# Four latent-cross-attention layers over 64 sequences on one core: masks, padded keys, value matmuls, weight transfers and the order of the work changed

## Chip, cores and metric

One NeuronCore of a Trainium2 chip runs the whole program. The metric is the device time of one execution in microseconds (us). Engines: PE (TensorE, matmul), DVE (VectorE), ACT (ScalarE), POOL (GpSimd), SP (SyncE, which only issues transfers here).

## What is computed

Four layers are applied to x (64 sequences x 64 tokens x 256) with a context of 64 tokens per sequence. Cut to what matters:

```
x = L0(ctx, x, mask)   # 16 heads of 16: softmax(q k) v over ctx and x together (128 keys; the
                       # context's masked keys get no weight), out, + x, norm, gelu MLP, + x
x = L1(x, ctx)         # RWKV block: token shift, five mixes, r k v w g, state scan
                       #   s = k v + w s,  out = r (u k v + s), group norm, gate, feed-forward
x = L2(x, ctx)         # one head of 256: x + alpha * softmax(q k) v Wo
x = L3(x, ctx, amask)  # 32 query heads of 8 on 8 key/value heads, + additive mask, out, + x, norm
```

Everything is float32.

## The kernel before

The 64 sequences are worked in 16 tiles of 4 (256 tokens). Each tile goes through three parts: A (L0), B (the RWKV mixing of L1) and C (the feed-forward of L1, then L2 and L3), as lists of named stages (`STAGES`). The string `ORDER`, written out by hand as 82 letters, says from which part the next stage comes; `AHEAD` lets A work two tiles and B one tile ahead of C. So one iteration of the program holds the stages of A for tile t+2, of B for t+1 and of C for t, mixed as ORDER has them: 18 iterations, the first with A alone, the second with A and B, then 14 with all three, one with B and C, one with C. All five engines walk the same sequence (`run`), each doing its share of each stage in that order and waiting on semaphores for the others. There is no scheduler: where a stage stands in ORDER sets what stands behind a wait on every engine, SP's transfers among them.

PSUM: banks 0 to 3 hold the scores and then the values and sums of both attentions (`max`, `exp`, `value` stages, A and C by turns), banks 4 and 5 belong to B, and banks 6 and 7 are a ring for all dense matmuls of A and C (`USES`, `SLOT`, `spare`, `full`, `read`): a matmul of slot k waits until slot k-2 has been read.

The stages that the text below speaks of:

- `q0`, `k0`, `v0` (L550, 552, 559 on PE): the projections of A. ACT writes `kT` from `k0`.
- `max0` (`max_scores`, L417): scores of two sequences, 16 matmuls in four row groups of 32 rows; then 8 more (L410 `pw<-m,wa`) add `m0`, -1e30 for a masked key, to the first 64 keys. DVE takes maxima (L1112). `turn0` (L578) transposes them, `exp0` makes the scores again, transposed, with -max added; ACT exponentiates (L837) with the mask as bias. `value0` (`values`) makes sums and values, DVE divides (L1117, L1120) to `tA`, `out0` multiplies by the output weights, `norm0` adds x on DVE (L1202), squares on ACT (L887), takes the root on POOL (L1014, L1016) and scales on ACT to `a2` (L891), which `zturn` transposes on PE (L399 `pw<-wa,a`). `up` (L610, four stages, gelu on ACT at L899) and `down` (L616) are the MLP.
- `mix2` (L513): five mixes of part B. Mix j multiplies 32 rows of `thB` in row group f % 4, f = `MIX[j]` = 2, 0, 1, 3, 4, into bank 4 or 5 by turns; DVE finishes each (L1241) and POOL adds (L1052). `mixes(0, 1)` and `mixes(2, 3)` interleave the matmuls of two mixes, `mixes(4)` is alone.
- `ruk`, `scan` 0 to 7, `sum`, `oturn` in B: SP copies v to eight places (`copy_v`), POOL makes the outer products (L1029), DVE scans (L1262), POOL multiplies with r (L1065), PE sums (`gather`).
- `k3`, `v3` in C: keys and values of the third attention, the one of L3. ACT makes four padded copies of the keys for the four places of a head in a group of 32 rows (`kz3`, L987). `v3` multiplies twice (L774), once for each half of the output rows, and DVE copies the heads into padded places. `max1`: PE (L410 `pw<-kz,q3T`), DVE adds the mask (L1108) and takes maxima (L1112). `x3turn` transposes (L399 `pw<-wa,c`), ACT copies to `tC` (L976), `q3` multiplies.

PE itself waits at the start for the weights `wa` and for DVE's preparation of them, whose last step halves `fv` (L1377).

Of the kernel before, what the change touches and what calls it, by code (L numbers as in the profile page):

```python
# [7 lines left out]
I32 = mybir.dt.int32  # L8
# [4 lines left out]
P = 128  # L13
# [19 lines left out]
WEIGHTS_A = [("ident", P), ("q0", 2 * C), ("k0", 2 * C), ("v0", 2 * C), ("o0", 2 * C), ("vec", 64), ("fv", 2 * C), ("ones0", 48), ("ones3", 64), ("pick", 32),  # L33
             ("top", P), ("eye", 32), ("o3", 2 * C)]
# [43 lines left out]
ORDER = "AABACBABCCBCABCABCABBCBBCABBAABABACBACBCBCBBCCBBACBAABBCABABACBBCBBBCBBBACCBACCBCB"  # L78
# [48 lines left out]
def build(nc, h_d, x_d, mask_d, maskt_d, amask_d, s0_d, e0_d, wa_d, wb_d, nat_d, rows_d, out_d):  # L127
# [4 lines left out]
    with ExitStack() as ctx:  # L132
# [249 lines left out]
        def _(pe):  # L382
# [154 lines left out]
            def part_a(name, i, t):  # L537
# [166 lines left out]
            def part_c(name, i, t):  # L704
# [765 lines left out]
```

## Time and profile before

| | before |
|---|---|
| median of 3 runs | 1628.97 us (1628.13 to 1629.14) |
| the profiled execution | 1628.69 us |
| its span, first to last instruction | 1626.5 us |
| mean granted clock of PE | 0.964 of full speed |
| busy: PE, PE weight loads | 1459.5 us (90%), 1119.1 us (69%) |
| busy: DVE, POOL, ACT | 958.1 (59%), 649.4 (40%), 626.7 us (39%) |
| chain that ended last, by engine | PE 71%, DVE 10%, ACT 7%, POOL 7%, issue 3%, DMA 2% |

The span is what the profiler saw between the first and the last instruction; the execution's own time is 2.2 us longer. Busy times of matmuls are modelled and overlap, so the time of a step on PE is better read as the distance from its start to the next start. A timeline row gives the start (us from the span's start), the length of the group, engine, source line, operation, what it writes and reads, its shape and how many records it has (an f32 matmul has two), and in brackets the idle time ahead of it with what ended it.

### The profile page before, as it was taken

Reading aid. Unit: us, or ns where it says so; the run is one execution under the profiler, and the core shown is the slowest. Engines: PE = TensorE matmul, PEld = TensorE weight load, DVE = VectorE, ACT = ScalarE, POOL = GpSimd, SP = SyncE. Lnnn points to the kernel's source line nnn. Section 1 sums busy time; section 2 is a strip of 40 time slices with the busy share of each in tenths; the row PEclk is TensorE's granted clock in tenths of the full one; section 3 lists DMA queues with packets and bytes.
Section 4 is the critical chain, followed back from the end, with each engine's and each line's share of the span. In section 5 each row is a group of like instructions: output and inputs, shape, how many; then the busy total and the mean of one; then the engine's idle time right before and its main releaser. Section 6 shows DMA issues by size and latency. Waiting matters only on the chain.

```text
span 1626.5 us, 45176 instructions
## 1 busy us (share of the span) xinstructions
PE 1459.5 (90%) x19704; PEld 1119.1 (69%) x19704; DVE 958.1 (59%) x1913; ACT 626.7 (39%) x1367; POOL 649.4 (40%) x604
## 2 busy tenths in 40 slices
PE   6777999999999999999999999999899999997664
PEld 4665767777777767777776777777676777775443
DVE  1244576665657576674757666575756656573733
ACT  2332444434343443534344343434344343433221
POOL 1043344525344453525335452533445253443410
PEclk9898999999999999999999999999999999997877
DMA  8021130404022040403113040311304040221300
GB/s 293 11 41 29 22 67 15 77 25 77 25 31 58 16 76 24 77 25 54 34 24 74 18 77 25 70 28 28 65 14 77 25 77 24 34 31 22 49 7 8
DMA packets 83093, 75.27 MB, mean 46 GB/s; under 512 B 37201, under 2 KB 72145, under 8 KB 82513
## 3 DMA queue, kind: packets, MB, share of 16 engines
q1 hardware_dynamic: 82896, 72.39, 22.2%
q8 instruction: 156, 2.56, 0.6%
q14 instruction: 41, 0.33, 0.1%
HBM read 34.61 MB, written 4.19 MB: 24 GB/s over the span
## 4 chain that ended last, share of the span: by engine, by line
PE 71%; DVE 10%; ACT 7%; POOL 7%; issue 3%; DMA 2%; SPq 0%; DVEq 0%; POOLq 0%; ACTq 0%
PE pw L410 21%; PE pw L388 14%; PE pw L394 7%; PE pw L610 6%; PE pw L616 6%; PE pw L559 3%; DVE c L1117 3%; POOL ab L1065 3%; PE pw L513 3%; POOL ab L1029 2%; PE pw L399 2%; PE pw L552 2%; ACT qz L861 2%; PE pw L729 2%; ACT ptC L839 1%
## 5 line engine op out<-in xcount | busy, mean ns | idle before, releaser
L1029 POOL TENSOR_TENSOR ab<-big,kvrg 128x504 f32<-128x504 f32 x128 | 161.2, 1259 | 115.9 <-DMA big<-kvrg 86.3
L1065 POOL TENSOR_TENSOR ab<-ab,kvrg 128x512 f32<-128x512 f32 x128 | 162.7, 1271 | 67.9 <-DVE ab L1262 67.6
L1262 DVE TENSOR_TENSOR_SCAN ab<-pw,ab 128x256 f32<-128x256 f32 x256 | 158.6, 671 | 48.4 <-ACT ab L947 45.9
L1052 POOL TENSOR_TENSOR big<-big,xaB 128x512 f32<-128x512 f32 x80 | 101.4, 1269 | 166.4 <-DVE big L1241 165.2
L610 PE MATMUL pw<-tA,wb 128*128 128x256 f32 x512 | 123.6, 397 | 3.7 <-DVE tA L1206 3.1
L388 PE MATMUL pw<-big,wb 128*128 128x256 f32 x512 | 125.8, 389 | 0.0
L616 PE MATMUL pw<-wb,ptA 128*128 128x256 f32 x512 | 118.1, 384 | 0.0
L1112 DVE TENSOR_REDUCE mx<-pw 128x8 f32<-128x1024 f32 x64 | 75.2, 1216 | 72.3 <-PE pw L410 72.3
L610 PEld LDWEIGHTS pw<-tA,wb 128*128 128x128 f32 x512 | 98.4, 197 | 27.8 <-issue 12.4
L1117 DVE RECIPROCAL a<-pw 128x256 f32<-128x256 f32 x32 | 56.1, 1752 | 103.0 <-PE pw L410 103.0
L616 PEld LDWEIGHTS pw<-wb,ptA 128*128 128x128 f32 x512 | 96.9, 192 | 15.2 <-issue 2.4
L388 PEld LDWEIGHTS pw<-big,wb 128*128 128x128 f32 x512 | 92.1, 190 | 18.9 <-POOL big L1052 4.6
L1014 POOL TENSOR_TENSOR vtmp_A<-mv_A,eps 128x2 f32<-128x2 f32 x16 | 3.2, 197 | 254.5 <-DVE mv_A L1132 254.5
L839 ACT ACTIVATE ptC<-pw 128x1024 f32<-128x1024 f32 x64 | 62.0, 1021 | 88.5 <-PE pw L410 88.5
L837 ACT ACTIVATE ptA<-pw,mk 128x1024 f32<-128x1024 f32 x64 | 67.8, 1111 | 63.1 <-PE pw L410 63.1
L899 ACT ACTIVATE ptA<-pw,wa 128x256 f32<-128x256 f32 x128 | 53.7, 471 | 99.0 <-PE pw L610 99.0
L388 PE MATMUL pw<-tC,wb 128*128 128x256 f32 x256 | 71.7, 428 | 16.6 <-ACT tC L976 13.4
L1241 DVE SCALAR_TENSOR_TENSOR big<-pw,wa,sxB 128x256 f32<-128x256 f32 x160 | 66.8, 475 | 32.5 <-PE pw L513 32.5
L410 PE MATMUL pw<-mT,wa 32*64 32x128 f32 (+1 forms) x3072 | 75.9, 274 | 4.4 <-issue 4.4
L1108 DVE TENSOR_TENSOR ptC<-pw,m 128x1024 f32<-128x1024 f32 x64 | 74.9, 1211 | 7.3 <-PE pw L410 6.8
L1112 DVE TENSOR_REDUCE mx<-ptC 128x16 f32<-128x1024 f32 x64 | 75.0, 1214 | 1.1
L388 PEld LDWEIGHTS pw<-tC,wb 128*128 128x128 f32 x256 | 50.7, 208 | 32.3 <-DVE v3s L1339 14.6
(216 smaller groups left out, 3082.6 us busy)
## 6 DMA issues: line engine op xcount, KB each, us to landing
big<-kvrg SPq DMA_DIRECT2D x256, 128.0 KB, 4.1
hT<-in_h SPq DMA_DIRECT2D x16, 512.0 KB, 4.4
m<-in_amask SPq DMA_DIRECT2D x96, 64.0 KB, 2.3
wb<-in_wb SPq DMA_DIRECT2D x1, 5120.0 KB, 22.6
a<-in_x SPq DMA_DIRECT2D x16, 256.0 KB, 4.2
xB<-in_x SPq DMA_DIRECT2D x16, 256.0 KB, 2.8
result<-c SPq DMA_DIRECT2D x16, 256.0 KB, 2.1
m<-in_mask SPq DMA_DIRECT2D x16, 128.0 KB, 2.5
```

The source lines that it names most:

```text
L388: last = mm(out[:, m, :], weight(k)[:, m * P:(m + 1) * P], rhs(k), start=(k == 0), stop=(k == 1))
L394: last = mm(out[:, t, :], lhs(k, t), weight(k), start=(k == 0), stop=(k == ks - 1))
L410: return mm(out, lhs, rhs, start=first, stop=last, skip_group_check=True)
L610: last = mm(kn(bank(k))[:, m, :], w("w1", c)[:, mt * P:(mt + 1) * P], tA[:, c, :], start=(c == 0), stop=(c == 1))
L616: last = mm(bank(k)[:, 0:C], hid[:, c, tok(i)], w2[:, c, :], start=(c == 0), stop=(c == 7))
L839: last = A(pt[1][p][:, 2 * j:2 * j + 2, :], pw[:, 2 * j:2 * j + 2, :], ACT.Exp)
L1029: G.tensor_tensor(ab[i % 4][:, :, :, 1:S], vx[i % 3].rearrange("p j (b s) -> p j b s", b=NB)[:, :, :, 0:S - 1], k, ALU.mult).then_inc(kv_p ...
L1052: G.tensor_tensor(v, v, xaB[:, :, :, 1:S + 1].rearrange("p k b s -> p (k b) s"), ALU.add).then_inc(xm_ok, 1)
L1065: G.tensor_tensor(ab[i % 4][:, :, :, :], st[i % 2][:, :, :, :], r, ALU.mult).then_inc(pd_ok, 1)
L1112: V.tensor_reduce(mx[:, 2 * j:2 * j + 2, g * p:g * p + g], src[:, 2 * j:2 * j + 2, :].rearrange("p r (g s) -> p r g s", g=g), AXX, ALU.max ...
L1117: V.reciprocal(rc[layer][:, p, :], ps[(1, 2)[p]][:, 0:2 * P]).then_inc(o_rc, 1)
L1262: last = V.tensor_tensor_scan(st[i % 2][:, j, :, :].rearrange("p b s -> p (b s)"), kn(b5)[:, i // 4, :], ab[i % 4][:, j, :, :].rearrange(" ...
```

## The change

Masked keys: in place of adding -1e30 by matmuls, DVE compares the mask (`gone`) and copies over each masked context key in `kT` the key of the first latent position (column S), by a predicated copy. The maximum is then one over real keys; the weights still get their mask in `exp0`. Padded keys: ACT writes one copy `k3S`, POOL makes the four padded ones from it. `v3`: each product is made once, and DVE copies it to both halves, in eight pieces. `mixes` becomes `mix`: the mixes are no longer interleaved. Weights: `wa` comes in two transfers, PE waits for the first only, and no longer for `set_pool` and `set_dve`; the halving of `fv` moves into `fold_weights`. And ORDER is another string.

```diff
-WEIGHTS_A = [("ident", P), ("q0", 2 * C), ("k0", 2 * C), ("v0", 2 * C), ("o0", 2 * C), ("vec", 64), ("fv", 2 * C), ...
+WEIGHTS_A = [("vec", 64), ("q0", 2 * C), ("k0", 2 * C), ("ident", P), ("ones0", 48), ("ones3", 64), ("pick", 32), ("top", P), ("eye", 32),
+             ("v0", 2 * C), ("o0", 2 * C), ("fv", 2 * C), ("o3", 2 * C)]
...
-ORDER = "AABACBABCCBCABCABCABBCBBCABBAABABACBACBCBCBBCCBBACBAABBCABABACBBCBBBCBBBACCBACCBCB"
+ORDER = "AABACBABBCCBBABCCCBCBBCABBBCBABCBBBCACCBAABBCAAACABBBCBABAACBBCABBBCBBBACCBACCACBB"
...
-            sp.dma_start(wa[:, :], wa_d).then_inc(ld_w, 16)
+            sp.dma_start(wa[:, 0:ca["v0"][0]], wa_d[:, 0:ca["v0"][0]]).then_inc(ld_w, 16)
             load_context(0)
+            sp.dma_start(wa[:, ca["v0"][0]:na], wa_d[:, ca["v0"][0]:na]).then_inc(ld_v, 16)
...
-                if layer == 0:
-                    for i in range(2):
-                        b = 2 * p + i
-                        for r in range(4):
-                            last = into(ps[r][:, 256 * i:256 * i + 256].rearrange("p (k s) -> p k s", k=2)[:, :, 0:S], w("top")[group(r), :],
-                                        m0[group(r), b, :].unsqueeze(1).broadcast_to([32, 2, S]), False, i == 1)
...
-            def mixes(*js):
-
+            def mix(j):
+
+                f = MIX[j]
+                g = group(f % 4)
                 for m in range(2):
-                    for j in js:
-                        f = MIX[j]
-                        g = group(f % 4)
-                        last = mm(kn((b4, b5)[j % 2])[:, m, :], w("m2", f // 4)[g, m * P:(m + 1) * P], thB[g, f // 4, :], start=True, stop=True)
-                        if m == 1:
-                            last.then_inc(m2_ps, 1)
+                    last = mm(kn((b4, b5)[j % 2])[:, m, :], w("m2", f // 4)[g, m * P:(m + 1) * P], thB[g, f // 4, :], start=True, stop=True)
+                last.then_inc(m2_ps, 1)
...
-                        pe.wait_ge(*read(SLOT["k0", 0, t]))
-                        pe.wait_ge(*read(SLOT["k0", 0, t] + 1))
-                        pe.wait_ge(m0_ok, t * 2 + 1)
+                        pe.wait_ge(k0_ok, t + 1)
...
-                        mixes(0, 1)
+                        mix(0)
+                        mix(1)
...
                     for b in range(NB):
-                        for e in range(2):
-                            for c in range(2):
-                                last = mm(bank(k)[64 * e:64 * e + 64, b * 64:(b + 1) * 64], hT[t % 3][:, c, b, 0:S], w("v3", c),
-                                          start=(c == 0), stop=(c == 1))
+                        for c in range(2):
+                            last = mm(bank(k)[64 * (b % 2):64 * (b % 2) + 64, b // 2 * 64:b // 2 * 64 + 64], hT[t % 3][:, c, b, 0:S], w("v3", c),
+                                      start=(c == 0), stop=(c == 1))
...
-                        for made in ("q3", "k3"):
-                            pe.wait_ge(*read(SLOT[made, 0, t]))
+                        pe.wait_ge(*read(SLOT["q3", 0, t]))
+                        pe.wait_ge(kz_ok, t + 1)
...
             pe.wait_ge(ld_w, 16)
-            pe.wait_ge(set_pool, 2)
-            pe.wait_ge(set_dve, 7)
...
-                    for v in range(4):
-                        last = A(kz3[:, :, v, :], seqs(bank(k)[:, 0:NT]), ACT.Identity, bias=kb3m[:, v:v + 1], scale=vec("sub", v))
-                    last.then_inc(read(k)[0], 2)
+                    A(k3S[:, :], bank(k)[:, 0:NT], ACT.Identity, bias=vec("kb3")).then_inc(read(k)[0], 2)
...
+                elif name == "k3":
+
+                    pool.wait_ge(*read(SLOT[name, i, t]))
+                    for v in range(4):
+                        last = G.tensor_scalar(kz3[:, :, v, :], k3S[:, :].rearrange("p (b s) -> p b s", b=NB), vec("sub", v), None, ALU.mult)
+                    last.then_inc(kz_ok, 1)
...
-                    V.tensor_scalar(m0[:, :, :], m0[:, :, :].bitcast(I32), 0.0, MASKED, ALU.is_equal, ALU.mult).then_inc(m0_ok, 1)
+                    V.tensor_scalar(gone[:, :, :], m0[:, :, :].bitcast(I32), 0.0, None, ALU.is_equal).then_inc(m0_ok, 1)
...
+                    dve.wait_ge(*read(SLOT[name, 0, t]))
+                    dve.wait_ge(*read(SLOT[name, 0, t] + 1))
+                    dve.wait_ge(m0_ok, t * 2 + 1)
+                    for m in range(2):
+                        last = V.copy_predicated(kT[:, m, :, 0:S], gone[:, :, :], kT[:, m, :, S:S + 1].broadcast_to([P, NB, S]))
+                    last.then_inc(k0_ok, 1)
...
```

What ORDER does to the instructions shows in three places. The line numbers of the changed kernel differ by a few, so the pieces are printed apart; a row is a group of equal instructions.

PE around `zturn` (L399 and L406 `pw<-wa,a`) in a full iteration. Before, from `x3turn` to `turn1` (L792):

```order
L399 MATMUL pw<-wa,c 128x128 x4
L388 MATMUL pw<-tC,wb 128x256 x4
L410 MATMUL pw<-ab,wb 32x256 x4
L399 MATMUL pw<-wa,a 128x128 x4
L410 MATMUL pw<-kz,q3T 128x256 x8
L610 MATMUL pw<-tA,wb 128x256 x8
L410 MATMUL pw<-ab,wb 32x256 x4
L410 MATMUL pw<-kz,q3T 128x256 x8
L610 MATMUL pw<-tA,wb 128x256 x8
L616 MATMUL pw<-wb,ptA 128x256 x8
L792 MATMUL pw<-wa,mx 128x128
```

and now, from the first `sum` to `turn1`:

```order
L417 MATMUL pw<-ab,wb 32x256 x4
L395 MATMUL pw<-tC,wb 128x256 x4
L401 MATMUL pw<-wa,tA 128x256 x4
L417 MATMUL pw<-kz,q3T 128x256 x8
L406 MATMUL pw<-wa,a 128x128 x4
L417 MATMUL pw<-ab,wb 32x256 x4
L417 MATMUL pw<-kz,q3T 128x256 x8
L609 MATMUL pw<-tA,wb 128x256 x12
L792 MATMUL pw<-wa,mx 128x128
```

`out0` (L401 `pw<-wa,tA`) has moved down to one step before `zturn`; of the four `up` stages three are left between the two `max1` stages and `turn1`, and `down0` (L616) has left.

PE around `value0` (from L410 `pw<-ptA,wa`), before, from the second `exp0` on:

```order
L410 MATMUL pw<-qz,kT 128x128 x16
L410 MATMUL pw<-mT,wa 128x128 x16
L388 MATMUL pw<-big,wb 128x256 x4
L671 MATMUL pw<-thB,wb 128x256 x2
L410 MATMUL pw<-ptA,wa 32x256 x8
```

and now:

```order
L417 MATMUL pw<-qz,kT 128x128 x16
L417 MATMUL pw<-mT,wa 128x128 x16
L774 MATMUL pw<-wb,hT 64x64 x8
L406 MATMUL pw<-wa,c 128x128 x4
L417 MATMUL pw<-ptA,wa 32x256 x8
```

Between `exp0.1` and `value0` stood `pr` and `pw2` of B; now `v3` and `x3turn` of C stand there.

POOL from the copy of the residual (L1070) to `norm0` (L1010) in the changed kernel, whose rows L1025 and L1061 are the outer products and the products with r:

```order
L1070 TENSOR_TENSOR c<-c,rows 128x512
L1025 TENSOR_TENSOR ab<-big,kvrg 128x8x63
L1061 TENSOR_TENSOR ab<-ab,kvrg 128x512
L1025 TENSOR_TENSOR ab<-big,kvrg 128x8x63
L1061 TENSOR_TENSOR ab<-ab,kvrg 128x512
L1075 TENSOR_SCALAR kz<-k3S,wa 128x4x64 x4
L1025 TENSOR_TENSOR ab<-big,kvrg 128x8x63
L1061 TENSOR_TENSOR ab<-ab,kvrg 128x512
L1025 TENSOR_TENSOR ab<-big,kvrg 128x8x63
L1061 TENSOR_TENSOR ab<-ab,kvrg 128x512
L1010 TENSOR_TENSOR vtmp_A<-ssq_A,eps 128x2
```

The four `kz` passes are new, between the second and the third pair; before, `norm0` stood ahead of the first product (L1065 there), and now it stands behind the fourth.

## Rows read from the trace of the kernel before

**Rows 1.** Windows: stretch, length, busy us of each engine (instructions), PEclk, DMA, GB/s
```profile
155.60:1463.60 1308.00, 1244.07 (x17221) 957.85 (x17219) 830.45 (x1647) 545.92 (x1191) 563.48 (x514) 0.99 0.23 43
...
769.90:773.30 3.40, 3.40 (x16) 1.68 (x15) 1.02 (x3) 0.94 (x3) 1.61 (x3) 0.50 0.83 142
```

**Rows 2.** Waits of PE over the span: us in total, times, longest
```profile
PE pw L399 <- ACT kz L987: 17.8, 16, 1.6
...
PE pw L394 <- DVE tC L1120: 9.2, 16, 0.9
```

**Rows 3.** PE timeline (start, length, operation, count); last row: a group by shape
```profile
822.36 0.62 PE L410 MATMUL pw<-m,wa 32*128 32x128 f32 x16
822.80 1.04 PE L513 MATMUL pw<-thB,wb 32*128 32x256 f32 x8
...
837.37 1.02 PE L513 MATMUL pw<-thB,wb 32*128 32x256 f32 x4
...
844.51 1.07 PE L410 MATMUL pw<-mT,wa 32*128 32x128 f32 x32
...
853.97 1.89 PE L394 MATMUL pw<-wa,tA 128*128 128x256 f32 x8
...
859.30 1.20 PE L774 MATMUL pw<-wb,hT 128*64 128x64 f32 x32
...
L513 PE MATMUL pw<-thB,wb 32*128 32x256 f32 x320 | 50.9, 384 | 1.0 <-ACT thB L913 1.0
```

**Rows 4.** PE timeline, same iteration, later; in brackets: idle before, releaser
```profile
862.08 0.66 PE L399 MATMUL pw<-wa,c 128*128 128x128 f32 x4 [1.58 <-ACT kz L987]
...
866.20 0.71 PE L399 MATMUL pw<-wa,a 128*128 128x128 f32 x4
866.84 1.15 PE L410 MATMUL pw<-kz,q3T 32*128 32x256 f32 x16
868.45 3.69 PE L610 MATMUL pw<-tA,wb 128*128 128x256 f32 x16 [0.46 <-DVE tA L1206]
...
877.28 3.62 PE L616 MATMUL pw<-wb,ptA 128*128 128x256 f32 x16
880.73 0.27 PE L792 MATMUL pw<-wa,mx 128*128 128x128 f32 x1
```

**Rows 5.** Timeline of DVE in that iteration
```profile
867.85 0.46 DVE L1206 TENSOR_SCALAR tA<-pw,wa 128x256 f32<-128x256 f32 x1
868.22 2.34 DVE L1108 TENSOR_TENSOR ptC<-pw,m 128x1024 f32<-128x1024 f32 x2
...
872.86 2.42 DVE L1262 TENSOR_TENSOR_SCAN ab<-pw,ab 128x256 f32<-128x256 f32 x4
...
877.56 2.34 DVE L1112 TENSOR_REDUCE mx<-ptC 128x16 f32<-128x1024 f32 x2
```

**Rows 6.** Timeline of ACT in that iteration
```profile
845.71 2.12 ACT L837 ACTIVATE ptA<-pw,mk 128x1024 f32<-128x1024 f32 x2 [1.06 <-PE pw L410]
...
859.20 0.91 ACT L891 ACTIVATE a<-a,rstd_A 128x256 f32<-128x256 f32 x2 [1.61 <-POOL rstd_A L1016]
...
867.33 1.28 ACT L899 ACT_TABLE_LOAD   x1
```

**Rows 7.** Timeline of POOL in that iteration
```profile
827.71 2.13 POOL L1071 TENSOR_SCALAR m<-m 128x768 f32<-128x768 f32 x1
...
861.76 1.27 POOL L1065 TENSOR_TENSOR ab<-ab,kvrg 128x512 f32<-128x512 f32 x1
```

**Rows 8.** Timeline of DVE and PE at the start of the program
```profile
7.70 0.36 DVE L1364 TENSOR_SCALAR qb0m<-wa 128x2 f32<-128x2 f32 x2 [7.70 <-DMA wa<-in_wa]
...
10.01 2.47 PE L388 MATMUL pw<-hT,wa 128*128 128x256 f32 x5 [10.01 <-DVE wa L1377]
```

**Rows 9.** PE timeline, in the filling pass and in an earlier iteration
```profile
124.15 1.08 PE L410 MATMUL pw<-ab,wb 128*32 128x256 f32 x8 [8.27 <-POOL ab L1065]
...
769.07 2.99 PE L388 MATMUL pw<-tC,wb 128*128 128x256 f32 x8 [0.84 <-ACT tC L976]
```

More of the change, by code:

```diff
@@ L30 @@
 GN = 2 + 2 + 3 * NEWTON
-WEIGHTS_A = [("ident", P), ("q0", 2 * C), ("k0", 2 * C), ("v0", 2 * C), ("o0", 2 * C), ("vec", 64), ("fv", 2 * C), ("ones0", 48), ("ones3", 64), ("pick", 32),
-             ("top", P), ("eye", 32), ("o3", 2 * C)]
+WEIGHTS_A = [("vec", 64), ("q0", 2 * C), ("k0", 2 * C), ("ident", P), ("ones0", 48), ("ones3", 64), ("pick", 32), ("top", P), ("eye", 32),
+             ("v0", 2 * C), ("o0", 2 * C), ("fv", 2 * C), ("o3", 2 * C)]
 WEIGHTS_B = [("w1", 2 * HID), ("w2", 8 * C),
@@ L186, in build @@
         m0 = sb("m0", [P, NB, S])
+        gone = sb("gone", [P, NB, S], I32)
         mkint = sb("mkint", [S, NB], I32)
@@ L218, in build @@
         q3T = sb("q3T", [P, NB, 2, S])
+        k3S = sb("k3S", [P, NT])
         kz3 = sb("kz3", [P, NB, 4, S])
@@ L252, in kn @@
             return bank[:, :].rearrange("p (k n) -> p k n", k=2)
+        ld_v = sem("ld_v")
         ld_w, ld_wb, ld_nat, ld_rows, ld_e = sem("ld_w"), sem("ld_wb"), sem("ld_nat"), sem("ld_rows"), sem("ld_e")
@@ L278, in build @@
         e_ps, e_sb, o_ps, o_rc, o_sb = sem("e_ps"), sem("e_sb"), sem("o_ps"), sem("o_rc"), sem("o_sb")
+        k0_ok = sem("k0_ok")
+        kz_ok = sem("kz_ok")
         m0_ok, m3_ok, a_rd = sem("m0_ok"), sem("m3_ok"), sem("a_rd")
@@ L418, in max_scores @@
                             for r in range(4):
-                                into(ps[r][:, (2 * i + k) * P:(2 * i + k + 1) * P], qz[group(r), k, b, :, :],
-                                     kT[group(r), k, b, :], i + k == 0, False)
+                                last = into(ps[r][:, (2 * i + k) * P:(2 * i + k + 1) * P], qz[group(r), k, b, :, :],
+                                            kT[group(r), k, b, :], i + k == 0, i + k == 2)
                     else:
@@ L554, in part_a @@
                 elif name == "v0":
+                    if t == 0:
+                        pe.wait_ge(ld_v, 16)
                     for b in range(NB):
@@ L641, in part_b @@
                         pe.wait_ge(m1_sb, t * 2 + 2)
-                        mixes(0, 1)
+                        mix(0)
+                        mix(1)
                     elif i == 2:
                         pe.wait_ge(m2_mx, t * 5 + 2)
-                        mixes(2, 3)
+                        mix(2)
+                        mix(3)
                     elif i == 4:
                         pe.wait_ge(m2_mx, t * 5 + 3)
-                        mixes(4)
+                        mix(4)
                 elif name == "pv":
@@ L1175, in fold_weights @@
             def fold_weights():
+                dve.wait_ge(ld_v, 16)
+                V.tensor_scalar(w("fv"), w("fv"), 0.5, None, ALU.mult)
                 dve.wait_ge(ld_wb, 16)
@@ L1335, in part_c @@
                     for e in range(2):
-                        g = slice(64 * e, 64 * e + 64)
-                        for v in range(2):
-                            o = (2 * v + e) * W3
-                            last = V.tensor_copy(v3[g, :, :, v, o:o + W3],
-                                                 bank(k)[g, 0:NT].rearrange("p (b r x) -> p b r x", b=NB, r=2)[:, :, :, o:o + W3])
+                        for h in range(2):
+                            for v in range(2):
+                                o = (2 * v + e) * W3
+                                last = V.tensor_copy(v3[64 * e:64 * e + 64, h:NB:2, :, v, o:o + W3],
+                                                     bank(k)[64 * h:64 * h + 64, 0:P].rearrange("p (b r x) -> p b r x", b=2, r=2)[:, :, :, o:o + W3])
                     last.then_inc(read(k)[0], 2)
@@ L1375, in _ @@
                 c = vec0 + VEC[name][0]
-                V.tensor_scalar(wa[:, c:c + 2], wa[:, c:c + 2], 0.5, None, ALU.mult)
-            V.tensor_scalar(w("fv"), w("fv"), 0.5, None, ALU.mult).then_inc(set_dve, 1)
+                last = V.tensor_scalar(wa[:, c:c + 2], wa[:, c:c + 2], 0.5, None, ALU.mult)
+            last.then_inc(set_dve, 1)
             run(dve, stage)
```

## The prediction

> **What bounds the kernel now.** I read three views, in this order. The windows come first [rows 1]: the stretch in which all three parts run (from the first matmul of `q0` in one iteration to that of the fourteenth after it) is 1308.0 us long, so 93.4 us an iteration, and TensorE (PE) is busy for 1244.07 us of it, 95%, while VectorE (DVE) has 830.45 us, ACT 545.92 and POOL 563.48. So in these 14 iterations PE's own list sets the time, and what it waits for is only some 4.5 us each. Before this stretch lie 155.6 us of filling, after it 1626.5 - 1463.6 = 162.9 us of emptying: these two are bound by the chains of single parts. Second, PE's waits [rows 2]: 17.8 us for the four `kz` activations of ACT and 9.2 us for the second quotient `tC` are the largest that come in every iteration, 16 times each. Third, the order in time of one iteration: on PE [rows 3, 4] for what each step costs, counted from start to next start since the modelled ends overlap, and on DVE, ACT and POOL [rows 5 to 7] for what PE will have to wait for in the new order.
>
> **The change, part by part** (per iteration, where not said otherwise).
>
> 1. *Mask matmuls of `max0` go.* One of the two groups runs from 822.36 to 822.80 [rows 3]: 0.44 us, two of them 0.9 us. PE is the bound, so all of it counts: -0.9.
>
> 2. *`v3` half as often.* Its 32 records take 1.20 us [rows 3]; half go: -0.6. DVE copies eight small pieces in place of four; they lie in DVE's free time and I cost them at nothing; without that cover they would add under 1 us ahead of the third scan.
>
> 3. *`mix(0)`, `mix(1)` written apart.* This is no gift. Before, the two stand interleaved, one in row group 64 to 95, one in 0 to 31: four matmuls (8 records, since each f32 matmul is two passes) take 1.04 us, while the two matmuls of the last mix (4 records) take 1.02 us alone [rows 3]. So the interleaved ones run in pairs: with 0.38 us for the last pass, pair follows pair after (1.04 - 0.38) / 3 = 0.22 us. Written apart, the four passes of one mix follow each other in one row group, and only the last of them can overlap the first of the other: seven slots in place of four, 3 x 0.22 = 0.65 us. Nothing of before shows the new order; its bounds are 0 (the array pairs them all the same) and 1.0 us (no overlap at all, twice the row). I take 0.65, since order of issue is what the rows show; two such places make +1.3. The Trainium skill (TensorE: Matmul & The Clock Gate, "The mechanism" of part 3) says that the queue may pull weight loads ahead but that matmuls stay strictly first in, first out; by that rule the 0 end falls away.
>
> 4. *Weights in two transfers, PE no longer waits for DVE's preparation.* DVE starts at 7.70 us when the whole of `wa` is there, PE at 10.01 us, behind DVE's last scaling [rows 8]. The first part is 43% of the bytes (1520 of 3568 columns), and the context follows it in the queue. I let PE start at about 7.4 us: once -2.6. In the filling pass of part A alone the two mask groups also stand on the chain: -0.9, together -3.5 once.
>
> 5. *Predicated copies on DVE.* Two of 128x256 each iteration, after ACT's `kT`. Before shows none; near are DVE's 128x256 pass at 0.46 [rows 5] and a 128x1024 pass at 1.17, so 0.3 to 1.2 us each, and I take 0.45, its own size. They stand ahead of the DVE steps of `xturn`, whose `xin_ok` is what PE's `mix1` waits for; behind them DVE had 1.0 us of air before `cturn`, PE had some 0.8. So +0.3 on PE; the far end would be +1.5.
>
> 6. *`k3` on POOL.* ACT's four activations become one, so the two waits behind them go. In the printed iteration PE waits 1.58 us for `kz` before `x3turn` [rows 4] and 0.84 us for ACT's copy to `tC` after it [rows 9]. The second goes as well because `q3` now stands six steps after `x3turn`. The 0.54 us before `out1` (9.2 over 16 [rows 2]) go too, since `out1` now stands after `down1`, when DVE has both quotients, and so do 0.46 before `up` [rows 4] and 0.19 of small ones: 3.6 in this iteration. The mean bears it out, though the `kz` wait alone is 17.8 / 16 = 1.1: PE's whole idle time is (1308.0 - 1244.07) / 14 = 4.6, and I leave 0.8 to 1.0 of it for the waits at `k0` and `cturn`, where the order stays: -3.6. POOL gets four passes of 128x256. Its one-input pass of 128x768 takes 2.13 us [rows 7], so 0.71 each, 2.8 in all; the far end is that of a 512-wide two-input pass, 1.27 each, 5.1. `max1` needs them some 3 us after they end, so they are hidden, but they sit in POOL's list between the second product and the fifth outer product.
>
> 7. *The order.* Two places get worse.
>  - *`value0`.* ACT needs 2.12 us for the exponentials of `exp0.1` and begins 0.2 after PE [rows 3, 6]: PE may go on 2.4 us after its last matmul. Before, `pr` and `pw2` stood between (3 us). Now `v3` (0.6) and `x3turn` (0.65) do: +1.1.
>  - *`out0`, `zturn`, `max1`, `turn1`.* The path from `out0` to `zturn` goes over DVE, ACT, POOL, ACT: before, PE's `out0` ended at 855.86 and `a2` was there at 860.11 [rows 3, 6], 4.3 us later, with PE coming back at 866.20. Now only `max1.0` (1.1 us) stands between: PE waits 3.2 us. Then `turn1` needs all maxima. From `max1.0` DVE has two additions (2.34), two maxima (2.34), `tA` (0.46), two scans (2.42 for four passes), and additions and maxima once more [rows 5]; back to back they go from 868.22 to 879.9, 11.65, and with `tA`, which stood ahead of them, 12.1. With `max1.0`'s 1.1 and 0.3 of releases that is 13.5 us from `max1.0` to `turn1`. Before, the same window is 13.9 us (866.84 to 880.73) and nearly full: its PE work is 13.4. Now `down0` (3.45) and one `up` (1.8) leave it and `zturn` (0.65) enters [rows 4]: 8.8 us of work in 13.5 us. The wait for `zturn` lies inside, so it is not added: +4.7.
>  ACT also loads its tables twice more (gelu between two exponentials), 1.28 us each [rows 6]; both lie under PE's 3 us long `exp1` steps and cost nothing; without that cover, up to 2.6.
>
> Sum for one iteration: -0.9 - 0.6 + 1.3 + 0.3 - 3.6 + 1.1 + 4.7 = +2.3 us; times 14 = +32.
>  Filling with A and B: before, PE stands 8.27 us before the first `sum` [rows 9], since `exp0.1` and the mask loads behind it stand ahead of `pr`, `pg` and the copies of v. Now they stand behind; `pg` ends some 8 us earlier, and part of that is given back in `zturn` and `sum`: -5 (0 to -8). Emptying: the `k3` waits go, mixes and POOL passes come: 0 (±3).
>  Sum: 32 - 3.5 - 5 = +23.5. The profiled execution took 1628.69 us (span 1626.5 and 2.2 around it), the median of the runs is 1628.97, the same within 0.02%; I predict **1652 us**.
>
> **The rivals.**
> - *Faster: the DVE window does not bind.* Everything rests on 13.5 us from `max1.0` to `turn1`. If DVE gets through it beside PE (its additions starting on half of the scores, or PE arriving at `max1.0` late, in the shadow of another wait), the sum is 2.3 - 4.7 = -2.4 an iteration: 1628.7 - 34 - 8.5 = **1586**. It decides at 3.0 us: if the window's stall is smaller than that, 14 iterations cost less than the 8.5 us won at the start. For it: PE is the only full engine and loses 1.5 us of work and 3.6 us of waits. Against: DVE's passes are back to back in before, in the same order [rows 5]. With smaller misses in its direction (mixes paired, waits half as long) it fills 1586 to 1622. Chance 0.22.
> - *Slower by the clock.* In before, behind the wait of 0.84 us at 769.07, the granted clock is 0.50 (the 1.2 GHz level) from 769.9 to 773.3 [rows 1], and the eight records there take 2.99 us [rows 9] where eight such take 1.9; such a stretch costs half its length, 1.7 us. The mean of 0.99 over the 1308 us leaves room for 4 to 11 of them (0.5 to 1.5% of 1308, over half of 3.4) [rows 1]. Now each has waits of some 3.2 and 1.5 us in this place. If each gets such a stretch, and it does not fall inside the DVE window, where it is free, this adds up to 14 x 1.7 = 24: **1676**. The Trainium skill (TensorE: Matmul & The Clock Gate, "HAM oscillation") describes just that, a wait in every turn of a loop and a throttled stretch after each; its rule makes this rival the likelier one, the slack before `turn1` (13.5 - 3.2 - 8.8 = 1.5 us) speaks against. Chance 0.17, in which I put the far ends of steps 5 and 6 too.
> - *It does nothing.* Gains and new waits cancel, since the old stalls (3.6) and the new one (4.7) are of one size: 1626 to 1632, chance 0.06.
>
> **How the numbers follow.** The forecast has 0.55, its own range 1636 to 1668 (0.7 us an iteration to either side, and the filling's bounds). Leaving 0.1 out at either end, the range is 1612 to 1680. A measurement tells 0.2%, 3 us, from no change. Faster: 0.22; same: 0.05; slower: 0.73.
>
> **What would show it.** In the profile after, the first matmul before 8 us; no mask group; L513's groups of four matmuls at 1.6 to 1.7 us; no wait for `kz` before `x3turn`; a PE wait of 3 us before the transposes of `a2`, then 1 to 2 us before `turn1`, released by DVE's maxima; 1.1 us before `value0`; an iteration of 95 to 96 us. PE's busy time hardly changed (16 iterations: -14, -10, +21) with a longer span would show that waits, not work, did it. I am wrong if `turn1` follows `up` without a wait, or if `zturn` finds `a2` ready.

## The result, and the profile after

| | before | after |
|---|---|---|
| median | 1629.06 us (4 runs, 1628.13 to 1630.76) | 1660.09 us (4 runs, 1656.53 to 1662.9) |
| ratio to before | | 1.0178 [1.0154, 1.0202] |
| profiled execution, its span | 1628.69 us, 1626.5 us | 1660.78 us, 1659.0 us |
| mean granted clock of PE | 0.964 | 0.946 |
| one iteration with all three parts | 93.4 us | 95.7 us |

The change makes the kernel 31 us slower. PE's busy time tells little: 1469.1 us in place of 1459.5. The windows of the kernel after, with the length, then the busy us of PE, PE's weight loads, DVE, ACT and POOL, the granted clock, the DMA share and GB/s:

```profile
152.50:1396.00 1243.50, 1161.39 (x15367) 889.61 (x15366) 788.71 (x1608) 519.81 (x1093) 561.20 (x530) 0.97 0.23 43
879.70:886.50 6.80, 5.14 (x31) 3.05 (x32) 6.33 (x9) 2.87 (x6) 3.39 (x4) 0.50 0.42 77
876.30:891.30 15.00, 11.13 (x70) 7.91 (x69) 13.94 (x17) 5.57 (x15) 8.32 (x8) 0.77 0.24 43
```

The first row is thirteen full iterations, from `q0` to `q0`: 95.65 us each, where [rows 1] gave 93.4. ([rows 1] ends at 1463.6, where part A has no tile left and so no `q0`; between the first matmuls of `k0` before also has thirteen full iterations, 93.45 us each, so its mean stands.) PE idles (1243.5 - 1161.39) / 13 = 6.3 us in each, before 4.6, and its clock is 0.97 where it was 0.99. The other two rows lie in one iteration, of which this is the PE timeline (start, length, operation, count, in brackets the idle time before and what ended it):

```profile
865.96 0.73 PE L774 MATMUL pw<-wb,hT 128*64 128x64 f32 x16
866.62 0.65 PE L406 MATMUL pw<-wa,c 128*128 128x128 f32 x4
868.33 1.07 PE L417 MATMUL pw<-ptA,wa 128*32 128x256 f32 x16 [1.05 <-ACT ptA L835]
...
872.69 1.99 PE L395 MATMUL pw<-tC,wb 128*128 128x256 f32 x8
874.52 1.89 PE L401 MATMUL pw<-wa,tA 128*128 128x256 f32 x8
876.34 1.15 PE L417 MATMUL pw<-kz,q3T 32*128 32x256 f32 x16
881.36 1.09 PE L406 MATMUL pw<-wa,a 128*128 128x128 f32 x4 [3.87 <-ACT a L889]
882.38 1.08 PE L417 MATMUL pw<-ab,wb 128*32 128x256 f32 x8
883.39 2.09 PE L417 MATMUL pw<-kz,q3T 32*128 32x256 f32 x16
885.41 6.00 PE L609 MATMUL pw<-tA,wb 128*128 128x256 f32 x24
891.25 0.27 PE L792 MATMUL pw<-wa,mx 128*128 128x128 f32 x1
891.45 0.64 PE L417 MATMUL pw<-ab,wb 128*32 128x256 f32 x8
892.60 1.17 PE L417 MATMUL pw<-q3T,kz 32*128 32x128 f32 x32 [0.51 <-ACT mT L991]
```

`x3turn` no longer waits for `kz` (1.58 us in [rows 4]), `value0` waits 1.05 us, `zturn` 3.87 us for `a2`. Then comes what [rows 9] showed only now and then: from 879.7 on, with PE idle since 877.5, the granted clock is 0.50 (the 1.2 GHz level) for 6.8 us, so `max1.1` takes 2.09 us where `max1.0` took 1.15 seven us earlier, and the three `up` take 6.00. `turn1` starts at 891.25 with no wait in brackets. Over the span, PE's waits in us, times and longest:

```profile
PE pw L406 <- ACT a L889: 59.4, 16, 5.2
PE pw L417 <- ACT ptA L835: 22.8, 18, 2.3
PE pw L792 <- DVE mx L1114: 13.8, 2, 7.9
```

The wait for `a2` comes 16 times, 3.7 us each. `turn1` waits for DVE's maxima in two places only, both where the program empties. DVE, ACT and POOL in the same stretch, each apart:

```profile
877.55 2.36 DVE L1110 TENSOR_TENSOR ptC<-pw,m 128x1024 f32<-128x1024 f32 x2 [0.36 <-PE pw L417]
879.95 2.34 DVE L1114 TENSOR_REDUCE mx<-ptC 128x16 f32<-128x1024 f32 x2
...
885.55 2.36 DVE L1110 TENSOR_TENSOR ptC<-pw,m 128x1024 f32<-128x1024 f32 x2 [0.16 <-PE pw L417]
887.94 2.35 DVE L1114 TENSOR_REDUCE mx<-ptC 128x16 f32<-128x1024 f32 x2
```

```profile
880.31 0.91 ACT L889 ACTIVATE a<-a,rstd_A 128x256 f32<-128x256 f32 x2 [2.17 <-POOL rstd_A L1012]
...
891.45 0.84 ACT L897 ACTIVATE ptA<-pw,wa 128x256 f32<-128x256 f32 x2 [0.89 <-PE pw L609]
892.18 0.28 ACT L991 ACTIVATE mT<-pw 128x128 f32<-128x128 f32 x1
```

```profile
870.13 3.63 POOL L1075 TENSOR_SCALAR kz<-k3S,wa 128x256 f32<-128x256 f32 x4
...
878.07 1.26 POOL L1061 TENSOR_TENSOR ab<-ab,kvrg 128x512 f32<-128x512 f32 x1
879.29 0.19 POOL L1010 TENSOR_TENSOR vtmp_A<-ssq_A,eps 128x2 f32<-128x2 f32 x1
879.56 0.72 POOL L1012 TENSOR_TENSOR rstd_A<-vtmp_A,power 128x2 f32<-128x2 f32 x1
```

DVE has its last maximum at 890.29. PE, slowed by the clock, comes to `turn1` only at 891.25, 0.96 us behind it, so the profile names no DVE wait: here PE and not DVE is last. From `max1.0` (876.34) to `turn1` it is 14.9 us. The printed iteration has one of the longer windows: over the thirteen full iterations this window is 13.4 to 15.0 us, 14.35 in the mean, and PE comes 0.06 to 1.4 us behind DVE's last maximum. The four `kz` passes of POOL take 3.63 us and end at 873.76, and `rstd_A` stands behind two outer products, the last of which ends at 879.3.

The low clock was also counted over the thirteen iterations: before it has 3 stretches of 3.4 us, 10.2 us in all; after it has 13, one in every iteration, six of 3.4 and seven of 6.8 us, 68.3 us in all. Each begins within the wait for `a2` or less than 2 us behind its end. With a long one the window from `max1.0` to `turn1` is 14.7 to 15.0 us, with a short one 13.4 to 14.5. At the busy share of the second windows row (5.14 of 6.8) they cost, as an estimate, 68.3 x 0.76 / 2 / 13 = 2.0 us an iteration.

### The profile page after: what moved, and what is told of

The parts are those of the page before. It is cut to its first block, busy times and chain, and to the rows that moved or that the text cites. A ratio compares the mean times of both kernels' runs of the same rounds, so it can differ in the third digit from the quotient of the medians.

```text
span 1659.0 us, 43797 instructions
## 1 busy us (share of the span) xinstructions
PE 1469.1 (89%) x18936; PEld 1121.4 (68%) x18936; DVE 978.7 (59%) x2009; ACT 637.6 (38%) x1347; POOL 696.7 (42%) x668
## 4 chain that ended last, share of the span: by engine, by line
PE 71%; POOL 11%; ACT 7%; DVE 6%; issue 3%; DMA 1%; SPq 1%; POOLq 0%; DVEq 0%; ACTq 0%
PE pw L417 19%; PE pw L395 13%; PE pw L609 7%; PE pw L615 7%; PE pw L401 7%; POOL ab L1061 3%; POOL ab L1025 3%; PE pw L560 3%; PE pw L513 3%; PE pw L406 3%; PE pw L730 2%; POOL kz L1075 2%; PE pw L551 2%; ACT ptA L835 2%; ACT qz L859 2%
## 5 line engine op out<-in xcount | busy, mean ns | idle before, releaser
L1025 POOL TENSOR_TENSOR ab<-big,kvrg 128x504 f32<-128x504 f32 x128 | 160.7, 1256 | 84.9 <-PE pw L417 49.7
L1061 POOL TENSOR_TENSOR ab<-ab,kvrg 128x512 f32<-128x512 f32 x128 | 162.4, 1270 | 63.5 <-DVE ab L1273 63.5
L1010 POOL TENSOR_TENSOR vtmp_A<-mv_A,eps 128x2 f32<-128x2 f32 x16 | 3.1, 196 | 317.8 <-DVE mv_A L1134 317.8
L609 PE MATMUL pw<-tA,wb 128*128 128x256 f32 x512 | 133.9, 420 | 0.7 <-DVE tA L1217 0.7
L1048 POOL TENSOR_TENSOR big<-big,xaB 128x512 f32<-128x512 f32 x80 | 92.2, 1177 | 91.3 <-DVE big L1252 90.1
L609 PEld LDWEIGHTS pw<-tA,wb 128*128 128x128 f32 x512 | 105.7, 213 | 29.5 <-issue 12.2
L395 PEld LDWEIGHTS pw<-big,wb 128*128 128x128 f32 x512 | 95.8, 195 | 17.5 <-issue 6.0
L417 PE MATMUL pw<-mT,wa 32*64 32x128 f32 (+1 forms) x3072 | 76.3, 275 | 2.3 <-issue 2.3
L1051 POOL TENSOR_TENSOR big<-kvrg 128x512 f32<-128x512 f32 x16 | 20.2, 1265 | 132.7 <-ACT kvrg L926 132.7
L859 ACT ACTIVATE qz<-pw,qb0m,wa 128x256 f32<-128x256 f32 x64 | 30.9, 563 | 115.8 <-PE pw L395 115.8
```

The costliest lines, as they stand in the source:

```text
L395: last = mm(out[:, m, :], weight(k)[:, m * P:(m + 1) * P], rhs(k), start=(k == 0), stop=(k == 1))
L417: return mm(out, lhs, rhs, start=first, stop=last, skip_group_check=True)
L609: last = mm(kn(bank(k))[:, m, :], w("w1", c)[:, mt * P:(mt + 1) * P], tA[:, c, :], start=(c == 0), stop=(c == 1))
L1025: G.tensor_tensor(ab[i % 4][:, :, :, 1:S], vx[i % 3].rearrange("p j (b s) -> p j b s", b=NB)[:, :, :, 0:S - 1], k, ALU.mult).then_inc(kv_p ...
L1048: G.tensor_tensor(v, v, xaB[:, :, :, 1:S + 1].rearrange("p k b s -> p (k b) s"), ALU.add).then_inc(xm_ok, 1)
L1061: G.tensor_tensor(ab[i % 4][:, :, :, :], st[i % 2][:, :, :, :], r, ALU.mult).then_inc(pd_ok, 1)
```

## The experiments

Ten kernels ran; each ratio is against the kernel before on the same chip. "Low clock" is the sum of the stretches at 0.50 in the full iterations. "First two" is the length of the pass of A alone and that of A and B, "last" all from the fourteenth and last full iteration to the end. Iteration, low clock, first two and last are those of the one execution that was profiled, measured between the first matmuls of `k0`, alike in all kernels; "us" is the median of all. The profiled execution of e3 was the fastest of its four (1661.3), so its iteration is a little short.

| kernel | us | ratio, 95% | iteration | low clock | first two | last |
|---|---|---|---|---|---|---|
| before | 1629 | 1 | 93.45 | 10.2 | 62.3, 81.5 | 254.3 |
| after | 1660.1 | 1.0178 [1.0154, 1.0202] | 95.66 | 68.3 | 63.4, 80.1 | 261.2 |
| e1, edits, old order | 1699.6 | 1.0439 [1.0415, 1.0463] | 98.37 | 102.4 | 61.6, 81.3 | 266.6 |
| e2, e1 with `kz` on ACT | 1630.0 | 0.9999 [0.9979, 1.0019] | 93.2 | 20.5 | 61.4, 83.9 | 261.2 |
| e3, new order alone | 1664.8 | 1.0233 [1.0207, 1.0258] | 95.57 | 61.4 | 59.0, 79.5 | 264.6 |
| e4, after, wait filled | 1628.9 | 0.9999 [0.9985, 1.0012] | 93.77 | 0 | 58.2, 76.8 | 262.0 |
| m1, before, mixes apart | 1633.0 | 1.0008 [0.9989, 1.0028] | 94.09 | 23.9 | 62.2, 80.8 | 252.6 |
| f2, e4 with `kz` on ACT | 1633.5 | 1.0022 [1.0004, 1.004] | 93.75 | 0 | 56.5, 77.3 | 265.3 |
| f3, e4 with `up3` early | 1626.0 | 0.9974 [0.9958, 0.9989] | 93.45 | 0 | 58.1, 78.1 | 261.2 |
| f4, wait half filled | 1640.0 | 1.0057 [1.0034, 1.0079] | 94.57 | 3.4 | 60.9, 77.5 | 260.7 |
| g1, before, start filled | 1631.4 | 1.001 [0.9991, 1.0029] | 93.5 | 17.1 | 58.7, 84.9 | 257.9 |
| g2, e2, start filled | 1627.0 | 0.998 [0.9963, 0.9997] | 93.16 | 20.5 | 60.9, 84.2 | 262.3 |

**e1: all edits, in the order of before.** In the kernel after:

```diff
-ORDER = "AABACBABBCCBBABCCCBCBBCABBBCBABCBBBCACCBAABBCAAACABBBCBABAACBBCABBBCBBBACCBACCACBB"
+ORDER = "AABACBABCCBCABCABCABBCBBCABBAABABACBACBCBCBBCCBBACBAABBCABABACBBCBBBCBBBACCBACCBCB"
```

> All of the change but ORDER, which is that of before. Theory A (the new order carries the whole loss, the other edits are gains on PE): 1600 to 1615 us, with the low-clock stretches of every iteration gone; the unknown in it is that POOL's four kz passes then stand right ahead of max1, which may wait for them by up to 3 us an iteration. Theory B (the edits cost, the POOL passes above all): 1630 to 1660 us.

The edits without the new order are worse than with it, which no theory had. PE's waits, and one iteration:

```profile
PE pw L417 <- POOL ab L1061: 74.9, 20, 8.3
PE pw L395 <- DVE v3s L1351: 30.7, 15, 2.1
```

```profile
795.20 2.57 PE L395 MATMUL pw<-tC,wb 128*128 128x256 f32 x8 [2.08 <-DVE v3s L1351]
801.57 1.08 PE L417 MATMUL pw<-ab,wb 128*32 128x256 f32 x8 [3.80 <-POOL ab L1061]
```

In the old order the 3.6 us of `kz` passes stand in POOL's list where a `sum` of PE waits for the product behind them. It waits 3.8 us. A second wait, 2.1 us in every full iteration, stands ahead of it: with no wait for `kz` any more, `q3` comes sooner and waits for DVE's eight copies of `v3` (e2 waits 0.84 us for ACT there). The low clock begins behind this second wait, at 796.5, and lasts past the first, to 806.7. So in the old order `k3` on POOL loses; this follows from e2, where only these passes went back.

**e2: e1 with the four `kz` passes on ACT again.**

```diff
-                    A(k3S[:, :], bank(k)[:, 0:NT], ACT.Identity, bias=vec("kb3")).then_inc(read(k)[0], 2)
+                    for v in range(4):
+                        last = A(kz3[:, :, v, :], seqs(bank(k)[:, 0:NT]), ACT.Identity, bias=kb3m[:, v:v + 1], scale=vec("sub", v))
+                    last.then_inc(read(k)[0], 2)
```

> As the run before, and the four padded key copies back on ACT. Theory A: the mask matmuls (0.9 us) and half of v3 (0.6 us) leave 14 full iterations, 2 to 3 us leave the start, so 1629 - 21 - 3 = 1605 us, with the kz wait of 1.1 us before x3turn still there. If the POOL passes are harmless in the old order, e1 is faster than this by 14 x 1 to 2 us; if they stall max1, e1 is slower.

1630.0, no gain at all from mask, v3 and weights, though mask and `v3` took 1.5 us of work from PE in each iteration; an iteration is only 0.25 us shorter. One row says where a part of it went:

```profile
PE pw L406 <- ACT kz L985: 24.6, 16, 2.0
```

1.54 us an iteration in place of 1.11 [rows 2]: `v3` stands right ahead of that wait, so most of what it saves PE is waited for. The mixes give back 0.2 (see m1), and the low clock took 20.5 us in place of 10.2, by the estimate above 0.3 an iteration. The rest, some 0.3 us, isn't traced. Thirteen iterations and the earlier start gain 3 us each, and the end of the program, 7 us longer, and the pass of A and B, 2.4 longer, take them back.

**e3: the kernel before in the new order, nothing else.**

> The kernel before with the new ORDER and nothing else. Theory A (order costs, edits gain): the loss of the change (31 us) and what the edits gain (about 24): 1675 to 1690 us. Theory B (edits cost): 1635 to 1650 us.

```profile
PE pw L399 <- ACT a L891: 55.1, 16, 5.1
```

The order alone carries the whole loss: 1664.8, the same wait for `a2` 16 times, 13 stretches of low clock. The edits are worth some 5 us on top of it by the medians, 9 by the ratios, whose intervals don't meet.

**e4: the wait filled.** Eight matmuls that nobody reads stand ahead of `zturn` in the kernel after; they write the bank that `zturn` then overwrites.

```diff
                 elif name == "zturn":
+                    for _ in range(8):
+                        mm(bank(k)[:, 0:C], ident, w("q0", 0), start=True, stop=True)
                     pe.wait_ge(n0_act, t * 2 + 2)
```

> The changed kernel with eight more matmuls of 128x256 (3.5 us at full clock) in PE's wait ahead of zturn, into the PSUM bank that zturn is about to fill; they change no result. Clock theory (each iteration loses 2 to 3 us in a low-clock stretch that follows this wait): the stretches go, an iteration falls by 1 to 2.5 us, 1625 to 1645 us though PE has 3.5 us more work an iteration. Window theory (DVE's 13.5 us from max1 to turn1 set the time, as the prediction had it): at most 0.3 us an iteration less, 1655 to 1662 us.

31 us faster with 3.5 us more PE work in every iteration. The timeline:

```profile
855.53 1.15 PE L417 MATMUL pw<-kz,q3T 32*128 32x256 f32 x16
856.61 3.72 PE L597 MATMUL pw<-wa 128*128 128x256 f32 x16
860.17 0.60 PE L406 MATMUL pw<-wa,a 128*128 128x128 f32 x4
860.70 0.64 PE L417 MATMUL pw<-ab,wb 128*32 128x256 f32 x8
861.26 1.15 PE L417 MATMUL pw<-kz,q3T 32*128 32x256 f32 x16
862.34 5.45 PE L611 MATMUL pw<-tA,wb 128*128 128x256 f32 x24
868.89 0.33 PE L794 MATMUL pw<-wa,mx 128*128 128x128 f32 x1 [1.10 <-DVE mx L1116]
```

`max1.1` is back at 1.15 us, `up` at 5.45, and no stretch of low clock is left in the full iterations. Only now does DVE's window show as a wait: `turn1` waits 1.10 us, and from `max1.0` (855.53) to `turn1` (868.89) it is 13.4 us, the same in all thirteen full iterations. The filling leaves the path to `a2` alone: `zturn` starts 4.68 us after `max1.0` in the mean, 4.70 without it. Of the 1.9 us that an iteration gets shorter, 1.0 lies in this window and 0.5 right behind it, where the kernel after waits for ACT's `mT`: PE comes late to the last `up`, ACT has its gelu pass to do first, and its copy of the maxima (L991) starts only at 892.18. Of the other 0.4, 0.2 are waits for which the trace shows no cause ("issue", 0.26 us an iteration after and 0.06 here).

**f4: half the filling**, four matmuls in place of eight.

> The changed kernel with four filling matmuls instead of eight, 0.9 of the 1.75 us. If the low clock of each iteration comes of PE's idle time ahead of zturn as a whole, half the filling leaves about 2.9 us idle of 3.9 and low stretches stay in some iterations: 1635 to 1655. If any work there is enough, 1627 to 1632 and no low stretch, as with eight. If the eight helped by something else than the clock (their place in the queue), half of the gain, near 1644, with the clock unchanged from the filled kernel's.

1640.0, between. A single stretch of low clock is left (3.4 us), so four matmuls do nearly all that eight do for the clock in the full iterations. Yet an iteration is 0.8 us longer than with eight:

```profile
PE pw L794 <- DVE mx L1116: 27.2, 15, 7.3
PE pw L406 <- ACT a L891: 24.9, 16, 2.7
```

`zturn` waits 1.6 us again, which costs nothing by itself since four matmuls (1.75 us) are missing, and the wait at `turn1` is about that of e4. The 0.8 us are not in every iteration: six of the thirteen take 93.6 to 93.7 us, and ten of e4's take 93.6. Four take 95.0 to 96.7, and in them lie the waits at L417 that nothing in the trace explains ("issue"), 6.9 us in all where e4 has 0.9; a fifth has the stretch of low clock (95.1). So half the filling does what all of it does for clock and window, and the rest of its loss comes with those waits, whose cause stays open; the expectation "1627 to 1632 if any work is enough" missed by it.

**m1: the mixes apart, on the kernel before.**

```diff
-                        mixes(0, 1)
+                        mix(0)
+                        mix(1)
```

(likewise for `mix(2)` and `mix(3)`, with the function `mix` of the change).

> The kernel before, with mix(0) and mix(1) (and mix(2), mix(3)) written apart as in the change, nothing else. Theory of the prediction (matmuls of two row groups start in the order in which they are written, so each mix runs its four passes one after the other): the groups at L513 take 1.6 to 1.7 us for eight records instead of 1.04, +1.3 us an iteration, +18 to 20 us in all: 1647 to 1650. Theory after the look at the changed kernel's rows (each row group works through its own matmuls, so pairs form again): eight records in 1.05 to 1.15 us, at most +0.2 us an iteration, 1629 to 1634.

```profile
827.96 1.13 PE L512 MATMUL pw<-thB,wb 32*128 32x256 f32 x8
835.84 1.13 PE L512 MATMUL pw<-thB,wb 32*128 32x256 f32 x8
```

1.13 us for eight records where [rows 3] has 1.04: +0.1 for each of the two places, not +0.65. Written one behind the other, the two mixes still run beside each other, each in its row group. (The iteration of the profiled execution is 0.64 us longer, with seven stretches of low clock in place of three, by the estimate above 0.4 of it; the medians can't be told apart, 1.0008 [0.9989, 1.0028].)

**f2: e4 with `kz` on ACT.** The edit of e2, in e4.

> The changed kernel with eight matmuls of 128x256 that nobody reads ahead of zturn (they fill PE's wait for a2), and with the four kz passes given back to ACT. If POOL's four passes (3.6 us) delay nothing in the new order, this stands beside the filled kernel with POOL (1628.9) or is slower by ACT's extra work: 1628 to 1635. If they delay the fifth outer product and with it the second scores, the 1.1 us that turn1 then still waits for DVE shrink: 1620 to 1627.

```profile
PE pw L794 <- DVE mx L1112: 27.1, 16, 7.3
```

The wait at `turn1` is that of e4 (26.9 us over 16), the iteration too. In the new order POOL's passes delay nothing that PE waits for in a full iteration; what f2 loses lies in the end of the program, 3.3 us.

**f3: e4 with the last `up` ahead of `turn1`.** One letter of ORDER moves:

```diff
-ORDER = "AABACBABBCCBBABCCCBCBBCABBBCBABCBBBCACCBAABBCAAACABBBCBABAACBBCABBBCBBBACCBACCACBB"
+ORDER = "AABACBABBCCBBABCCCBCBBCABBBCBABCBBBCACCBAABBCAAACABBBCBABAAACBBCBBBCBBBACCBACCACBB"
```

> The changed kernel with the same eight filling matmuls, and the last quarter of up (up3, 1.8 us of PE) moved ahead of turn1. If DVE's window of 13.4 us from max1.0 to turn1 is what PE still waits for there (1.10 us an iteration), 1.8 us of PE work moved into it fill that wait: -1.1 an iteration, -15 us: 1611 to 1618, faster than both kernels. Rival: the window moves with it (PE's tensors of the second scores or ACT's gelu are late instead), the wait goes to another place: 1625 to 1632.

```profile
861.30 7.17 PE L611 MATMUL pw<-tA,wb 128*128 128x256 f32 x32
868.31 0.27 PE L794 MATMUL pw<-wa,mx 128*128 128x128 f32 x1
...
869.66 1.17 PE L417 MATMUL pw<-q3T,kz 32*128 32x128 f32 x32 [0.51 <-ACT mT L993]
```

The wait at `turn1` is gone, and 0.51 us of it comes back as a wait for ACT's copy of the transposed maxima. An iteration is 0.3 us shorter in place of 1.1. Still, 0.9974 [0.9958, 0.9989] is the fastest kernel of this study and beats both others, by a quarter of a per cent over before.

**g1 and g2: the filling in the first two tiles only**, in the kernel before and in e2:

```diff
+                    for _ in range(8 if t < 2 else 0):
+                        mm(bank(k)[:, 0:C], ident, w("q0", 0), start=True, stop=True)
```

> The kernel before, with eight matmuls of 128x256 that nobody reads ahead of zturn in the first two tiles alone (the pass of part A alone and that of A and B), where PE waits 4.1 us for a2 and low clock follows. Theory (the clock, not the edits, is what the first two passes gain from): in the changed kernel the same filling made them 5.2 and 3.3 us shorter (63.4 to 58.2 and 80.1 to 76.8 us), so here -5 to -8 us in all, 1621 to 1624, with the steady iterations unchanged at 93.4. Rival: the old order has no wait of that size in the second pass, and the eight matmuls cost 1.5 to 3.5 us there; then 1625 to 1628.

> All edits in the order of before with the kz passes on ACT (the kernel that took 1630.0), with the same filling in the first two tiles. Theory: on top of the earlier start (3 us) the first two passes get 5 to 10 us shorter, 1620 to 1625. Rival: low clock stretches move to another place (this kernel had five in the full iterations and 88 us of them in the emptying), and it stays at 1627 to 1631.

g1: the pass of A alone gets 3.5 us shorter, the next 3.4 us longer. The old order gives the second pass its long wait at `sum`, ahead of the filling:

```profile
120.68 1.08 PE L410 MATMUL pw<-ab,wb 128*32 128x256 f32 x8 [8.28 <-POOL ab L1067]
121.69 2.93 PE L598 MATMUL pw<-wa 128*128 128x256 f32 x6
```

By then `a2` has long been there, and the eight matmuls are pure cost: the rival's mechanism, though 1631.4 lies above its 1625 to 1628 too. In g2 the first two passes change by only -0.5 and +0.3, and 1627.0, 0.998 [0.9963, 0.9997], is at the rival's edge, not the theory's.

## Why the prediction was right, and where it was not

Direction came out, and so did the size, 1652 forecast and 1660 measured, but the size in good part by luck. The forecast's +2.3 us an iteration had no term for the clock. e4 is the changed kernel with the wait filled and no low clock in the full iterations, and there the change costs +0.3 us (93.77 against 93.45); another 1.9 us, of the 2.2 measured, go away with the low clock. So the terms added up to some 2 us too much, mostly in the mixes, and the clock, put at nothing and argued down as a rival of chance 0.17, made up for it. Step by step:

1. *Mask matmuls, -0.9.* The group is gone. e2 and e3 can't tell it apart from the other edits; together these are worth 5 to 9 us in the new order.
2. *`v3`, -0.6.* The work shrank (0.73 us for its group at L774), but it stands ahead of a wait in either order. In e3, with the whole `v3`, the wait at `value0` is 0.58 us, with half of it 1.05: what PE saves it waits. The +1.1 at `value0` already had this in it, so the sum was right.
3. *Mixes, +1.3: wrong.* m1 measured +0.2. The forecast took the order of issue across row groups for the order of execution. The rows after show it does not hold across row groups; at L513 and L417, written as `mix(2)`, `mix(3)` and then the scores of `max0.1`:

```profile
839.44 0.49 PE L513 MATMUL pw<-thB,wb 32*128 32x256 f32 x2
839.47 0.48 PE L417 MATMUL pw<-kT,qz 32*128 32x128 f32 x2
839.76 0.59 PE L513 MATMUL pw<-thB,wb 32*128 32x256 f32 x3
839.99 0.37 PE L417 MATMUL pw<-kT,qz 32*128 32x128 f32 x1
```

 The scores start between the passes of the mixes. The Trainium skill (TensorE: Matmul & The Clock Gate, "The mechanism" of part 3) has matmuls strictly first in, first out; by it this would have cost 1.3, and here the measurement decides: within a row group perhaps, not between two.
4. *Weights in two transfers, start at 7.4 us.* Right:

```profile
7.21 3.75 PE L395 MATMUL pw<-hT,wa 128*128 128x256 f32 x8 [7.21 <-DMA hT<-in_h]
```

 PE starts 2.8 us earlier than in [rows 8] and now waits for the context. The rest of the start's gain, -0.9 in the pass of A alone, did not show (63.4 against 62.3 us). With the wait filled on both sides it is -0.5 (58.2 in e4, 58.7 in g1).
5. *Predicated copies, +0.3.* The two take 0.79 us together, 0.40 each, nearer to the 0.46 of [rows 5] than to the far end. No wait appeared at `mix1`, so they cost PE nothing.

```profile
829.45 0.79 DVE L1201 COPY_PREDICATED kT<-gone,kT 128x256 f32<-128x256 int32 x2
```

6. *`k3` on POOL, -3.6.* The `kz`, `tC`, `out1` and `up` waits went. The sum was right: PE's idle time outside `value0` and the window fell from 4.6 to 1.0 us (e4), though 0.6 of the 3.6 are `sum`'s waits for POOL, which the forecast did not name. The passes took 0.91 us each, not 0.71, and f2 shows them hidden. e1 shows the price without that cover, some 5 us an iteration with the low clock that comes with it; the forecast did not ask what POOL's list would do to `sum` in the old order.
7. *`value0`, +1.1.* 1.05 measured.
8. *DVE's window, 13.5 us and +4.7; the clock, 0.* Where the clock is full the window was right: 13.4 in e4, of which 1.05 us are wait at `turn1` and 3.5 filling, so 8.8 of work, the forecast's own figure. The wait at `zturn` was forecast at 3.2 and measured at 3.87 in the printed iteration, 3.56 in the mean. But that DVE's last maximum would be what PE waits for at `turn1` was wrong. The slack before `turn1`, forecast at 1.5 us and 1.05 in e4, from which the clock rival was argued down, was too small: the low clock stretched PE's work there to fill the slack and beyond. The window took 14.35 us in the mean, 1.0 more, and 0.5 came behind it at `mT`. That is the clock rival in its mechanism: it has a stretch in every iteration, and every iteration has one. Its price of 1.7 us was near what goes away in e4 (1.9, of which 1.5 can be placed); the time stayed below its 1676 because the other terms were too high. The Trainium skill (TensorE: Matmul & The Clock Gate, "HAM oscillation") describes a wait in each turn of a loop with a throttled stretch behind it; this trace agrees, with 13 stretches in 13 iterations, and e4, without the wait, has none. By that rule alone the time would have been the rival's 1676.
9. *Filling, -5.* -1.4 (81.5 to 80.1 us). PE's waits at `sum` in this pass fell from 11.3 to 1.3 us, but new ones came: 5.2 for `a2`, 3.5 for ACT's exponentials, 3.0 of a mix for DVE. Low clock goes with the `a2` wait here too: e4, with it filled, has 76.8 in this pass, 4.7 less than before.
10. *Emptying, 0 (±3): wrong.* The column "last" has +6.9, of which 2.2 are the fourteenth iteration's, so +4.7. The wait at `turn1` accounts for 3.2 of it: 13.8 us for its two in the waits shown above, 10.6 before. In all variants "last" is 258 to 267 us, except in before and m1 (254.3 and 252.6). e2 has +7 by the edits without the order, e3 +10 by the order without the edits, both with some 86 us of low clock there where before has 72. The kernel after has 73, so in it the low clock is not what made the end longer. And g1, which from the third tile on is the kernel before, has 257.9: up to 3.6 us of this may be the difference between two executions. Which edit does the rest was not tried, and stays open.

The sum of what was measured: start -2.8, first two passes +1.1 and -1.4, thirteen iterations 28.7, the rest +6.9, together +32.5, the difference of the spans. In an iteration the forecast had 1.1 too much for the mixes, 0.3 for the copies and 0.2 for the window, and it did not count that before itself loses some 0.3 us to its three low stretches, which e4 has not. Against that it had 1.9 too little for the clock and what comes with it: 2.3 against 2.2 by other parts. Over the program it had 8 us less, since the first passes gained less and the emptying lost.

## What to carry to other kernels

When an order is changed, read each engine's window at the new place, and then ask what the clock does behind every wait of several microseconds: here waits of 2.8 to 4.3 us cost another 1.5 to 1.9 us by the clock that goes with them, and an order that moves four short waits into one long one loses twice. A forecast whose number comes out still has to be taken apart: without e4 and m1 nobody would have seen that one term was too high and a rival's mechanism made up for it. A saving that stands just ahead of a wait is worth nothing until that wait is gone (`v3`), and moving passes to a less busy engine needs a look at that engine's list, not its total: POOL at 40% could take the same 3.6 us for nothing in the full iterations of one order and at 5 us an iteration in the other. Work that nobody reads, as long as the wait and on the waiting engine, is a cheap test of whether the clock or the wait costs.

## What the runs showed of the hardware

- Matmuls of different row groups of PE started out of the written order and beside each other; two mixes written apart (8 records) took 1.13 us, interleaved 1.04.
- Waits of 2.8 to 4.3 us for `a2` brought the 1.2 GHz level in 13 of 13 iterations; the same place with 3.5 us of work in it, in none; with 1.75 us of work and 0.8 to 2.1 of wait, in one.
- A predicated copy of 128x256 with an int32 mask took 0.40 us on DVE; POOL's scaling by a value per partition took 0.91 us for 128x256, more than its 128x768 pass with constants would give (2.13 / 3 = 0.71, [rows 7]).
